# Pixel refills issued by ScalarE, other PSUM banks for the embedding and the LoRA transposes, and the out-projection behind the transposes

## What is computed

```python
h = _L0_tok_ref(x, L0_tok_W)                              # patches @ W.T
h = _layernorm(h + _L0_attn_ref(h, ...))                  # qkv; (q k + q rel) causal softmax; v; w_proj
h = _layernorm(h + _L0_ffn_ref(h, ...))
# in _L0_ffn_ref
probs = jax.nn.softmax(xf @ Wg.T + bg, axis=-1)
top_w, top_idx = jax.lax.top_k(probs, TOPK)
combine = jnp.zeros((t, NUM_EXPERTS), x.dtype).at[jnp.arange(t)[:, None], top_idx].add(top_w)
h = jnp.einsum('td,erd->ter', xf, A) + ba
hw = h * combine[:, :, None]
delta = (jnp.einsum('ter,eor->to', hw, Bm) + combine @ bb) * SCALING
qkv = xf @ Wqkv.T + bqkv + delta                          # then plain attention and Wproj
```

## Time and profile before

| | |
|---|---|
| median of 3 runs | 452.47 us (450.39 to 453.39) |
| the profiled execution | 451.54 us, span 449.7 us |
| PE matmul busy | 408.8 us, 91% of the span |
| PE weight load busy | 360.2 us, 80% |
| VectorE busy | 294.5 us, 65% |
| ScalarE busy | 232.3 us, 52% |
| GpSimd (POOL) busy | 116.7 us, 26% |
| mean granted TensorE clock | 0.962 of full |
| DMA | 21.23 MB, mean 47 GB/s |

### The profile page before, as it was taken

One profiled execution on the slowest core, in us unless ns is written; L12 is line 12 of the kernel. 1 busy time (PEld: TensorE's weight loads), 2 busy tenths in 40 slices (PEclk: granted clock), 3 DMA queues, 4 the chain that ended last, 5 costly groups with the idle time before them and its releaser, 6 DMA issues.

```text
span 449.7 us, 13552 instructions
## 1 busy us (share of the span) xinstructions
PE 408.8 (91%) x5270; PEld 360.2 (80%) x5270; DVE 294.5 (65%) x783; ACT 232.3 (52%) x727; POOL 116.7 (26%) x237
## 2 busy tenths in 40 slices
PE   4993998999989999999999999999998999988974
PEld 3883886888878988889888898878987888886863
DVE  7042556756687767867587776786758758777662
ACT  1241456455465665555655556555555555454442
POOL 1011112230242223422333222343123321423122
PEclk9996899999999999999999999999999999998875
DMA  8552120101111111211111112110000000000010
GB/s 260 139 168 65 48 78 20 49 18 34 47 32 55 52 47 28 62 26 39 48 45 44 56 43 56 30 29 19 17 16 21 26 19 11 24 24 20 16 31 23
DMA packets 24377, 21.23 MB, mean 47 GB/s; under 512 B 16302, under 2 KB 20625, under 8 KB 24250
## 3 DMA queue, kind: packets, MB, share of 16 engines
q1 hardware_dynamic: 23738, 19.65, 15.4%
q10 hardware_dynamic: 576, 0.73, 0.5%
HBM read 13.13 MB, written 2.41 MB: 35 GB/s over the span
## 4 chain that ended last, share of the span: by engine, by line
PE 76%; ACT 8%; DVE 7%; issue 4%; DMA 3%; SPq 1%; POOLq 0%; POOL 0%; ACTq 0%; DVEq 0%
PE ps L414 11%; PE ps L484 10%; PE ps L497 7%; PE ps L472 7%; PE ps L508 6%; PE ps L519 5%; PE ps L449 4%; PE ps L453 4%; PE ps L451 4%; PE ps L436 3%; PE ps L438 3%; PE ps L520 3%; DVE mx L763 2%; PE ps L540 2%; DMA vbd<-vrow 2%
## 5 line engine op out<-in xcount | busy, mean ns | idle before, releaser
L763 DVE TENSOR_REDUCE mx<-ps 113x12 f32<-113x588 f32 x64 | 49.3, 770 | 81.0 <-PE ps L472 80.0
L378 POOL TENSOR_SCALAR kbd<-k,const 64x294 f32<-64x294 f32 x128 | 69.1, 549 | 99.5 <-ACT q L646 92.0
L667 ACT COPY pt<-ps 113x339 f32<-113x339 f32 x128 | 50.7, 445 | 52.1 <-PE ps L497 51.8
L385 POOL TENSOR_SCALAR shift<-mv,rstd 128x1 f32<-128x1 f32 (+1 forms) x50 | 13.2, 264 | 219.2 <-ACT rstd L702 219.2
L414 PE MATMUL ps<-tokw,xs 128*128 128x192 f32 (+1 forms) x300 | 58.0, 347 | 8.9 <-DVE res L791 5.0
L775 DVE TENSOR_REDUCE psum<-probs 113x12 f32<-113x588 f32 x64 | 48.4, 756 | 22.1 <-ACT probs L653 21.2
L414 PEld LDWEIGHTS ps<-tokw,xs 128*128 128x128 f32 (+1 forms) x300 | 51.9, 201 | 10.8 <-DVE res L791 6.5
L497 PE MATMUL ps<-const,probs 113*113 113x113 f32 x384 | 52.1, 274 | 2.7 <-DVE probs L784 2.4
L784 DVE TENSOR_TENSOR probs<-probs,rsum 113x588 f32<-113x588 f32 x64 | 51.3, 802 | 2.2
L508 PE MATMUL ps<-pt,vbd 113*32 113x49 f32 x1536 | 45.1, 231 | 8.3 <-DMA vbd<-vrow 6.9
L508 PEld LDWEIGHTS ps<-pt,vbd 113*32 113x32 f32 x1536 | 37.0, 152 | 19.0 <-issue 7.8
(11 more groups left out here) (79 smaller groups left out, 706.2 us busy)
## 6 DMA issues: line engine op xcount, KB each, us to landing
xs<-in_x SPq DMA_DIRECT2D x24, 384.0 KB, 4.3
vbd<-vrow SPq DMA_DIRECT2D x160, 18.4 KB
out<-o SPq DMA_DIRECT2D x24, 96.0 KB, 1.7
tail<-in_pos SPq DMA_DIRECT2D x1, 656.0 KB, 16.4
tokw<-in_tokw ACTq DMA_DIRECT2D x3, 192.0 KB, 3.5
w<-in_w SPq DMA_DIRECT2D x1, 472.5 KB, 9.9
xs<-in_x SPq DMA_DIRECT2D x3, 128.0 KB, 3.4
p<-in_p SPq DMA_DIRECT2D x2, 145.5 KB
```

Source lines behind the costliest of these rows:

```text
L378: last = nc.gpsimd.tensor_scalar(L.kbd[t % 2][:, e], L.k[:, :, at:at + T], kmask[:, e:e + 1], 1.0, ALU.mult, ALU.mult)
L667: nc.scalar.copy(pt[n % 2][:, 3 * half:3 * half + 3, :].rearrange("p g i -> p (g i)"), ps[0:PP, 2 + half, 0:3 * PP]).then_inc(pt_ready[hal ...
L763: nc.vector.tensor_reduce(mx[:].rearrange("p (b h) -> p b h", b=2), score_view, AX.X, ALU.max).then_inc(mx_ready, 1)
```

## The change

Three things move.

1. SyncE no longer issues pixels of blocks 1 and up. ScalarE issues those of blocks 1 to 4 at its start, with the first part of the positions ahead of them, and each refill right behind its own copy of the embedding (`take_h`). SyncE keeps block 0, weights, values and stores.
2. The embedding goes to PSUM bank 6 and waits for that bank's last user. The LoRA transposes go to bank 5 and wait for that bank's last user. The router product then waits for `hw_ready`, which VectorE sets, in place of `hwt_ready`, which ScalarE sets.
3. On TensorE both out-projections stand behind the transposes of h and of the probabilities.

```diff
@@ sync
-            load_x(1)
...
-            sp.dma_start(tail[64:128, 0:POS], pos_in[:, 0:POS]).then_inc(pos_loaded[0], 16)
-            load_x(2)
-            load_x(3)
...
-            load_x(4)
...
             for n in range(FIRST, SLOTS):
-                for b in embeds(n):
-                    if b + XS < BLOCKS:
-                        sp.wait_ge(emb_done, b + 1)
-                        load_x(b + XS)
@@ tensor, embed
-                    last = nc.tensor.matmul(ps[0:k, 5, 0:E], xs[:, b % XS, m, 0:k], tokw[:, m, :],
+                    last = nc.tensor.matmul(ps[0:k, 6, 0:E], xs[:, b % XS, m, 0:k], tokw[:, m, :],
@@ tensor, route
-                    pe.wait_ge(hwt_ready, b)
+                    pe.wait_ge(hw_ready, b)
@@ tensor, transpose_hw
-            def transpose_hw(b):
+            def transpose_hw(b, free):
                 k = tokens(b)
+                if free:
+                    pe.wait_ge(*free)
                 pe.wait_ge(hw_ready, b + 1)
-                nc.tensor.transpose(ps[0:1 + NE, 7, 128:128 + k], comb[0:k], ident[0:k, 0:k])
-                nc.tensor.transpose(ps[0:ER, 7, 0:k], hw[0:k], ident[0:k, 0:k]).then_inc(hwtr_done, 1)
+                nc.tensor.transpose(ps[0:1 + NE, 5, 128:128 + k], comb[0:k], ident[0:k, 0:k])
+                nc.tensor.transpose(ps[0:ER, 5, 0:k], hw[0:k], ident[0:k, 0:k]).then_inc(hwtr_done, 1)
+                return hwt_ready, b + 1
@@ tensor, the slot
+                for b in turns(n):
+                    bank6 = transpose_h(b, bank6)
+                if before:
+                    if n == 1:
+                        pe.wait_ge(zeros_ready, 2)
+                    transpose_probs(n - 1)
                 for b in out1(n):
...
-                for b in turns(n):
-                    bank6 = transpose_h(b, bank6)
-                if before:
-                    if n == 1:
-                        pe.wait_ge(zeros_ready, 2)
-                    transpose_probs(n - 1)
...
                 for b in embeds(n):
-                    bank5 = embed(b, bank5)
+                    bank6 = embed(b, bank6)
...
                 for b in routers(n):
-                    transpose_hw(b)
+                    bank5 = transpose_hw(b, bank5)
@@ scalar
+            act.dma_start(tail[64:128, 0:POS], pos_in[:, 0:POS]).then_inc(pos_loaded[0], 16)
...
+            for b in range(1, XS):
+                load_x(b)
...
-                nc.scalar.copy(h[0:k, b, :], ps[0:k, 5, 0:E]).then_inc(h_ready, 1)
+                nc.scalar.copy(h[0:k, b, :], ps[0:k, 6, 0:E]).then_inc(h_ready, 1)
+                if b + XS < BLOCKS:
+                    load_x(b + XS)
```

More of the change, by code:

```diff
@@ L307, in _ @@
         def _(sp):
-            def load_x(b):
-                sp.dma_start(xs[:, b % XS], x[b]).then_inc(x_loaded[b % XS], 16)
             for u in range(3):
                 sp.dma_start(xs[:, 0, 2 * u:2 * u + 2], x[0, :, 2 * u:2 * u + 2]).then_inc(x0_loaded[u], 16)
-            load_x(1)
             sp.dma_start(w1a[:], w1a_in).then_inc(w1a_loaded, 16)
             sp.dma_start(w1b[:], w1b_in).then_inc(w1b_loaded, 16)
-            sp.dma_start(tail[64:128, 0:POS], pos_in[:, 0:POS]).then_inc(pos_loaded[0], 16)
-            load_x(2)
-            load_x(3)
             sp.dma_start(p1[:], p1_in).then_inc(p1_loaded, 16)
@@ L622, in _, with load_x @@
             act.dma_start(const[:], const_in).then_inc(const_loaded, 16)
+            act.dma_start(tail[64:128, 0:POS], pos_in[:, 0:POS]).then_inc(pos_loaded[0], 16)
+            def load_x(b):
+                act.dma_start(xs[:, b % XS], x[b]).then_inc(x_loaded[b % XS], 16)
+            for b in range(1, XS):
+                load_x(b)
             def take_h(b):
@@ L692, in take_hw @@
                 act.wait_ge(hwtr_done, b + 1)
-                nc.scalar.copy(h1t[C:C + 1 + NE, 0, b % HB2, 0:k], ps[0:1 + NE, 7, 128:128 + k])
-                nc.scalar.copy(hwt[:, b % HB2, 0:k], ps[0:ER, 7, 0:k]).then_inc(hwt_ready, 1)
+                nc.scalar.copy(h1t[C:C + 1 + NE, 0, b % HB2, 0:k], ps[0:1 + NE, 5, 128:128 + k])
+                nc.scalar.copy(hwt[:, b % HB2, 0:k], ps[0:ER, 5, 0:k]).then_inc(hwt_ready, 1)
             def inverse_deviation(L, b):
```

## The result

The changed kernel has a median of 448.27 us over six runs (446.93 to 450.04); the kernel before, on the same chip, 452.5 (450.39 to 453.39, six runs). The ratio is 0.9907, with a 95% interval from 0.9878 to 0.9935. I had said 456, from 449 to 465, with the largest chance (0.47) on no change beyond 1%.

A forecast was written before the change was run, and what follows sets the result against it. PE's matmuls bound the kernel, busy 345.3 of 360.0 us. Terms 0.4 - 0.8 + 7.8 - 4.6 - 1.6 + 0.5 + 2.3 = +4.0 on 451.5 gave 455.5; with 0.9 for the median, 456 us, range 449 to 465.

The forecast's parts named there:

- Part 1: +0.4: Pixels issued by ScalarE: first values land 0.8 us later, clock's return shifts by -0.4; +0.4 us, from -3 to +2.
- Part 2a: Embedding in bank 6: its wait for VectorE goes, a wait for the v rows' copy comes; -0.8 and +7.8 us.
- -0.8: Embedding's wait for VectorE, 5.0 us in eight slots, goes, but only slots 22 and 30 keep the gain: -0.8 us.
- +7.8: Embedding waits for ScalarE's v copy: 1.3 us in five slots, 1.0 in slot 9, 0.3 in 3 and 4 together.
- most rests: In six slots with turns and an embedding, the embedding waits for ScalarE's late v copy, 1.3 us in five of them.
- the same chain takes it back: Slots 7, 15, 33, 41, 49: as in slot 25, the next slot waits for VectorE's probabilities, so no gain is kept.
- Part 2b: -4.6: LoRA transposes in bank 5: the router product's 4.4 us wait for ScalarE's copy goes; -4.6 us, 4.0 to 5.2.
- -1.6: Out-projection later, slots with turns: 1.0 us in 13, 21, 39, 47 and 0.6 in 5, 23, 31 are won.
- 0.5: Slots where the probabilities come last: out-projection no longer fills that wait; 0.4 stays in 57 and 58, 0.1 in 54: +0.5 us.
- 2.3: Tail: the later out-projection delays ScalarE's deviation and, behind it, the copy of the weighed values; +2.3 us, 1.4 to 2.8.
- the wait only changes its name: Slots without turns: the out-projection's wait for the weighed values passes to the probabilities' transposes, so nothing is won.
- The rival: Clock falls in the middle, at the new pauses of 1.3 to 1.5 us: three falls, 3.4 us each, 466 us; chance 0.17.

The follow-up runs named there:

- part 1 alone: Kernel before, with only the pixel refills of blocks 1 and up and the first positions issued by ScalarE: 452.43 us, ratio 0.9993.
- experiment 2: Changed kernel with the embedding put back into bank 5: 448.22 us; changed kernel with ScalarE's v copy ahead of the deviations: 441.19 us.
- 2a alone: Kernel before, with only the embedding moved to PSUM bank 6: 454.41 us, ratio 1.0032.
- experiment 1: Kernel before with one part each: pixels on ScalarE 452.43 us, embedding in bank 6 454.41, LoRA transposes in bank 5 446.27, out-projections behind the transposes 452.8.
- part 3 alone: Kernel before, with only both out-projections moved behind the transposes, in all slots: 452.8 us, ratio 1.0021.
- with turns only: Out-projection behind the transposes only in slots turning a block: kernel before 449.4 us, change 449.94, change with embedding in bank 5 443.87, change with split loads and v copy first 430.16.
- part 3 in slots with turns: Kernel before, with the out-projection moved behind the transposes only in slots that turn a block: 449.4 us, ratio 0.9922.

## Why the prediction was wrong, step by step

It said +4.0 us on the profiled execution's time. The changed kernel's slots and tail, falls left out, are about 2.4 us shorter.

- **Part 1: +0.4; measured 0.** Right in its main point, that the values land when they did: they start at 40.1 us in after and at 40.9 in part 1 alone, against 40.7 before; I had said 0.8 later, 41 to 42. That their wait is 8.3 us where I said about 8 is partly luck, since it depends on how early PE comes to them: in part 1 alone it is 10.7.
- **Part 2a: -0.8 and +7.8, so +7.0; measured within the change -1.2 and +8.3, so +7.1** (experiment 2). The step on which "most rests" held: six slots, 1.45 each in four of them where 1.3 was said. That in 7, 15, 41 and 49 "the same chain takes it back" is true only with part 3 beside it; for 2a alone it was wrong by 3 us (experiment 1), since I had read one slot's row and written it over six.
- **Part 2b: -4.6; measured -5.5**, mis-sized by 0.9 and outside its own 4.0 to 5.2. The wait of 1.34 us in slot 5 stands for 1.61; that the weight loads behind it come sooner too is my reading.
- **Part 3: -1.6 + 0.5 + 2.3, so +1.2; measured -3.7** (in part 3 alone). This is the step that failed, by 4.9 us. Two terms did it, by 3.5 and 2.2 us. In slots with turns I said 1.6 in seven; it is 5.1 in fifteen. The out-projection covers the v product's wait for its input in all fifteen, 0.27 us each, where I counted 0.2 in three; and in 13, 21, 39 and 47 the wait for the weighed values (0.27 us in slot 13) comes on top, where I counted it alone. And in slots without turns "the wait only changes its name" is wrong. Slot 14 of before has two waits, for `yt` and, since the transposes stand directly ahead of the values but for one product, for ScalarE's copy of them:

```profile
128.12 0.56 PE L519 MATMUL ps<-p,yt 96*128 96x192 f32 x2 [0.20 <-ACT yt L672]
128.52 0.49 PE L520 MATMUL ps<-p,yt 97*128 97x192 f32 x2
128.85 0.76 PE L497 MATMUL ps<-const,probs 113*113 113x113 f32 x6
129.44 0.38 PE L530 MATMUL ps<-const,h 128*96 128x128 f32 x2
129.99 0.70 PE L508 MATMUL ps<-pt,vbd 113*32 113x49 f32 x24 [0.16 <-ACT pt L667]
```

The out-projection, moved between the transposes and the values, covers that copy; in after no wait is left in the slot that the profile names, and the slot is 0.30 shorter:

```profile
122.75 0.85 PE L485 MATMUL ps<-const,probs 113*113 113x113 f32 x6
...
123.78 0.49 PE L508 MATMUL ps<-p,yt 97*128 97x192 f32 x2
124.11 0.38 PE L518 MATMUL ps<-const,h 128*96 128x128 f32 x2
124.42 0.70 PE L496 MATMUL ps<-pt,vbd 113*32 113x49 f32 x24
```

Such slots (14, 40, 48, 55, 56, 58, 62) give 2.2 us where I had nothing. The other two terms were off too and take 0.8 back. The loss in the slots bound by the probabilities was 2.0, not 0.5 (0.67 in 57 alone). The tail was +1.6, not +2.3; its mechanism is the one described, the copy of the weighed values behind the deviation, 4.24 us after the last transposes' start instead of 2.60:

```profile
434.98 1.45 PE L485 MATMUL ps<-const,probs 113*113 113x113 f32 x6 [2.19 <-DVE probs L784]
...
438.79 0.29 ACT L699 ACTIVATE lnv<-mv,eps_col 128x1 f32<-128x1 f32 x1 [1.88 <-DVE mv L803]
439.22 0.30 ACT L672 COPY yt<-ps 96x196 f32<-96x196 f32 x1
```

- **The clock.** The rival said three falls and 3.4 us each. There are two new ones in the profiled execution, but short ones, and one costs about 1.7. More: I set the sum against one execution and its clock. That of before had a clock loss of 17.1, below the mean of its kernel (20.4), that of after 21.1, above its own (18.8). Medians differ by 4.2 us, the two profiled executions by 1.5. The mean clock losses differ by 1.6 us, the slots and the tail by 2.4, and the two together come near the first number. This is no proof: the 18.8 is a mean of six executions from 16.5 to 21.9, and a difference in clock loss costs at most its own size. For the profiled pair the same addition fails, since -2.4 + 4.0 is +1.6 and not -1.5.

Put shortly: between +4.0 and -4.2 lie 8.2 us. Part 3 is 4.9 of them, part 2b 0.9, part 1 0.4 and part 2a -0.1, in all 6.1. Of the other 2.1 the clock can explain at most 1.6; the rest is within the 1.3 us that the interval of the ratio leaves to either side.

## What stays open

That part 3's longer waits lower the clock rests on the clock loss of four pairs of kernels, with part 3 everywhere and with turns only (24.7 and 20.7, 26.0 and 18.6, 15.7 and 10.5, but 18.8 and 17.6 in the change itself), and on where the falls stand in the profiled executions (last section), not on a run in which the pauses alone were changed. Why the wait for the v rows, in the change, goes with less clock loss (18.8) than its absence (26.0), though it is itself a pause of 1.2 us, no run settles. The traces show only that of 18 such waits of 0.9 to 1.2 us none was followed by a fall. Nor was a version run in which the out-projection stands behind the transposes with turns and where the LoRA copies are late, and in front elsewhere.

## What to carry to other kernels

Don't carry one slot's row over to others that look alike: measure in each the margin between the work that would be set free and what it waits for next; where the margins differ the gain does too. When a piece is moved, count both what it used to wait for and what it now covers, each adjacent wait for itself. And before moving any work around a wait, look at what stands ahead of the releasing instruction in its own engine's order: one copy put ahead of two small instructions was worth 7 us here, and three loads of 97 rows, each cut in 96 and 1, were worth 9, each of the two more than the whole change.

## What the runs showed of the hardware

- Issues on SyncE are held up behind a load of 97 rows: the next issue takes 6.3 us behind p1 and 10.9 us behind lora, and 0.58 and 0.33 us once these are split. The price is paid by whatever is issued behind, here the placements, which start at 23.5 us instead of 12.9.
- PE's clock falls in the middle of dense work. In the sixteen profiled executions there are 21 falls between 50 and 400 us, and each begins 0.9 to 3.5 us after the start of a pause of 0.9 to 1.7 us. But most such pauses bring none: PE idles that long 95 times there. Which wait it is matters. For the probabilities, at their transposes, it is 12 falls after 24 pauses, all in the six kernels with part 3 everywhere; for the LoRA copy, at the router product, 5 after 18; for VectorE, at the embedding, 1 after 18; for the v rows, at the embedding, none after 18. Why they differ is not shown.
- The same pause in the same slot brings a fall in some executions and none in others: the pause of 1.72 us shown for part 3 alone stands in the trace of part 3 in slots with turns too, without a fall, and the executions of part 3 alone differ from 22.5 to 29.6 us in clock loss. This goes with more than half of the spread of the runs (450 to 457 us for the kernel before), and two kernels whose slots differ by 7.1 us can have the same median.
